# Another order of the calls on all four compute engines of a fused two-layer kernel

## The reference: what is computed

```
x = LN(x + RG_LRU(x))      x = LN(x + FFN0(x))      x = LN(x + SSM(x))      x = LN(x + FFN1(x))

RG_LRU:  c = causal 4-tap depthwise conv(x);  r, i = sigmoid(c Wr), sigmoid(c Wi)
         a = a_base ** (8 r);  b = sqrt(1 - a*a) * (i * c)
         h[t] = a[t] h[t-1] + b[t]  (by cumulated, clipped logarithms)
         out = rmsnorm(h out_w) * norm_w
FFN:     relu(x W1 + b1) W2 + b2,  256 -> 1024 -> 256
SSM:     xi, z = x in_proj;  c = silu(causal 4-tap conv(xi));  B, C, dt = c x_proj  (16, 16, 1)
         dt = softplus(dt w + b);  for each of 16 states n:
         h_n[t] = exp(dt A_n) h_n[t-1] + dt B_n c;   y = sum over n of C_n h_n
         out = (y * silu(z)) out_proj
```

## Time and profile before

| | |
|---|---|
| runs | 959.28, 961.75, 962.03 us, median 961.75 |
| profiled execution | 961.2 us, its span 959.4 us |
| granted TensorE clock, mean | 0.916 |
| PE busy | 796.9 us, 83%, 2802 matmuls |
| DVE busy | 802.2 us, 84%, 1013 instructions |
| ACT busy | 671.6 us, 70%, 1345 instructions |
| POOL busy | 561.4 us, 59%, 468 instructions |

### The profile page before, as it was taken

The page is one execution under the profiler, slowest core; times in us unless marked ns, Lnnn a source line. Parts: engine busy times, 40 slices in busy tenths (PEclk is TensorE's granted clock), DMA queues, the critical chain, the costliest instruction groups (busy, mean ns, idle before and its releaser), DMA issues. The chain is left out here.

```text
span 959.4 us, 9608 instructions
## 1 busy us (share of the span) xinstructions
PE 796.9 (83%) x2802; PEld 528.2 (55%) x2802; DVE 802.2 (84%) x1013; ACT 671.6 (70%) x1345; POOL 561.4 (59%) x468
## 2 busy tenths in 40 slices
PE   2385867978987799999899999998998797787585
PEld 1264644736554556475647564756476546546464
DVE  5245566677799999999999999999999999989761
ACT  4347687588767865997699769876976685465452
POOL 0202457437836793789378937893776376565421
PEclk9597977989998889999999999999999799789597
DMA  9000000000100010001000100010000000000000
GB/s 315 12 23 22 23 1 22 1 1 0 56 1 0 1 42 13 0 1 59 8 1 1 60 1 0 1 46 0 1 1 27 1 1 1 23 0 1 22 1 22
DMA packets 10341, 19.49 MB, mean 20 GB/s; under 512 B 1457, under 2 KB 5297, under 8 KB 10289
## 3 DMA queue, kind: packets, MB, share of 16 engines
q1 hardware_dynamic: 10288, 18.88, 5.8%
HBM read 14.69 MB, written 4.19 MB: 20 GB/s over the span
## 5 line engine op out<-in xcount | busy, mean ns | idle before, releaser
L385 POOL TENSOR_TENSOR y<-y,hC 128x1024 f32<-128x1024 f32 (+3 forms) x140 | 280.1, 2001 | 77.3 <-DVE hC L1461 73.4
L1914 PE MATMUL pC<-w,hT 128*128 128x256 f32 x1024 | 232.4, 382 | 4.9 <-ACT hT L754 4.9
L819 ACT ACTIVATE dA<-dt,A_neg 128x512 f32<-128x512 f32 (+3 forms) x320 | 187.5, 630 | 54.3 <-DVE hs L1450 53.8
L1914 PEld LDWEIGHTS pC<-w,hT 128*128 128x128 f32 x1024 | 194.5, 191 | 36.7 <-issue 7.2
L1450 DVE TENSOR_TENSOR_SCAN hs<-dA,carry,pS 128x512 f32<-128x512 f32 (+3 forms) x192 | 193.4, 1008 | 18.1 <-ACT dA L819 10.4
L2037 PE MATMUL pS<-stack,sel 97*128 97x512 f32 (+3 forms) x320 | 148.0, 515 | 54.5 <-DVE hs L1450 54.0
L1435 DVE TENSOR_TENSOR pS<-u,pS 128x1024 f32<-128x1024 f32 (+3 forms) x160 | 159.8, 999 | 17.4 <-PE pS L2037 16.8
L1461 DVE TENSOR_TENSOR hC<-hs,pS 128x1024 f32<-128x1024 f32 (+3 forms) x160 | 157.5, 985 | 15.3 <-PE pS L2037 15.1
L1450 DVE TENSOR_TENSOR_SCAN hs<-dA,pS 128x512 f32<-128x512 f32 (+1 forms) x128 | 138.2, 1080 | 14.6 <-POOL carry L392 6.0
L754 ACT ACTIVATE hT<-pA,ffb_sb 128x512 f32<-128x512 f32 (+3 forms) x160 | 94.7, 599 | 59.2 <-PE pA L1907 58.9
L1907 PE MATMUL pA<-tg,w 128*128 128x512 f32 (+3 forms) x320 | 127.9, 538 | 7.7 <-ACT hT L754 6.3
(11 more groups left out here) (120 smaller groups left out, 1101.5 us busy)
## 6 DMA issues: line engine op xcount, KB each, us to landing
xt<-xT SPq DMA_DIRECT2D x6, 515.0 KB, 4.7
xtok<-x SPq DMA_DIRECT2D x6, 512.0 KB, 5.3
out<-x3b SPq DMA_DIRECT2D x6, 512.0 KB, 2.9
w<-w1a SPq DMA_DIRECT2D x1, 1024.0 KB, 8.3
w<-w2a SPq DMA_DIRECT2D x1, 1024.0 KB, 10.4
w<-w1b SPq DMA_DIRECT2D x1, 1024.0 KB, 8.3
w<-w2b SPq DMA_DIRECT2D x1, 1024.0 KB, 9.9
xt<-xT SPq DMA_DIRECT2D x2, 259.0 KB, 7.8
```

The costliest lines, as they stand in the source:

```text
L385: nc.gpsimd.tensor_tensor(y[:, :, 0:ch.T], so_far, hC[:, n % CRING, :, 0:ch.T], ALU.add).then_inc(S["y_sum"], 1)
L819: nc.scalar.activation(dA[:, k % ARING, 0:ch.T], dt[ch.side][:, h, 0:ch.T], ACT.Exp, scale=A_neg[:, h, n:n + 1]).then_inc(S["dA_ready"], 1)
L1914: mm = nc.tensor.matmul(dst[:, b * D:b * D + D], src(k, t0), w[:, k, :], start=k == 0, stop=k == nk - 1)
```

## The change

Each engine's `opening`, `entry`, `step` and `closing` get another order of their calls. The calls are the same ones with the same arguments, and the functions they call, their waits, the buffers, the loop over the steps and SP's program stay as they are. Steps -1 and 12 come out the same on all engines. In step 0 only ACT differs. The diff has 1,984 lines, nearly all of them moved calls; shown are the moves that the prediction speaks of.

ACT's `opening` (step 1; of the second half the conv and state_decay calls between the relus are left out here):

```
                 if gate is not None:
                     squares(gate)
+                if prep is not None:
+                    x_proj_high(prep)
+                if ahead is not None:
+                    conv_first(ahead)
+                if gate is not None:
                     over_rms(gate)
                 if prep is not None:
-                    x_proj_high(prep)
                     step_sizes(prep)
+                if ahead is not None:
+                    conv_tap(ahead, 1, prep)
+                if prep is not None:
                     state_decay(prep, 0)
                 if gate is not None:
                     normalize_gate(gate)
                 if prep is not None:
                     state_decay(prep, 1)
+                    state_decay(prep, 2)
                 if gate is not None:
                     to_channel_major(S["x1T_mm"], pA[0], x1T, S["x1T_ready"], gate, 0)
                     to_channel_major(S["x1T_mm"], pA[1], x1T, S["x1T_ready"], gate, 1)
-                if prep is not None:
-                    state_decay(prep, 2)
-                if ahead is not None:
-                    conv_first(ahead)
-                if gate is not None:
                     relu(0, gate, 0, tail)
-                if ahead is not None:
-                    conv_tap(ahead, 1, prep)
-                if gate is not None:
...
```

DVE's `entry`, around the recurrence (steps 2 and 3):

```
-                        state_output(scan, 2)
-                        state_scan(scan, 3, 1)
-                        state_input(scan, 4)
-                        state_scan(scan, 4, 0)
                         state_output(scan, 3)
                         state_scan(scan, 4, 1)
                         state_input(scan, 5)
-                if gate is not None:
-                    gate_input(gate)
-                if scan is not None:
                     state_scan(scan, 5, 0)
                     state_output(scan, 4)
                     state_scan(scan, 5, 1)
                     state_input(scan, 6)
-                if gate is not None:
+                    state_scan(scan, 6, 0)
+                    state_output(scan, 5)
+                if gate is not None:
+                    gate_input(gate)
                     scaled_input(gate)
-                    recurrence(gate)
-                if scan is not None:
-                    state_scan(scan, 6, 0)
-                if prep is not None:
-                    z_silu(prep, 0)
-                    z_silu(prep, 1)
-                if scan is not None:
-                    state_output(scan, 5)
+                if scan is not None:
                     state_scan(scan, 6, 1)
                     state_input(scan, 7)
                     state_scan(scan, 7, 0)
+                if gate is not None:
+                    recurrence(gate)
+                if prep is not None:
+                    z_silu(prep, 0)
+                    z_silu(prep, 1)
+                if scan is not None:
                     state_output(scan, 6)
                     state_scan(scan, 7, 1)
...
```

PE's `entry` (steps 2 and 3) moves out_proj1, and PE's `step` (4 to 9) moves the gate products; the order of the calls there, with the spreads that lie between left out:

```
 def entry(ahead, gate, prep, scan, tail):
     down(0, prep, 1, 0)
     down(0, prep, 1, 1)
     gate_mm(gate, 0, 0)
-    out_proj1(tail, prep)
     gate_mm(gate, 0, 1)
     gate_mm(gate, 1, 0)
     gate_mm(gate, 1, 1)
+    out_proj1(tail, prep)
     x2_transpose(prep, 0, gate)
...
 def step(ahead, gate, prep, scan, tail):
+    gate_mm(gate, 0, 0)
+    gate_mm(gate, 0, 1)
     down(0, prep, 1, 0)
     down(0, prep, 1, 1)
-    gate_mm(gate, 0, 0)
-    gate_mm(gate, 0, 1)
     gate_mm(gate, 1, 0)
     out_proj1(tail, prep)
     gate_mm(gate, 1, 1)
```

DVE's `step` (4 to 9), its first calls, with the ladder's calls left out:

```
 history(prep)
-add_ffn0(prep, 0, tail)
-add_ffn0(prep, 1, tail)
 readout(tail, gate)
 clip_log_decay(gate)
-add_ssm(tail, 0)
+add_ffn0(prep, 0, tail)
 log_A(gate)
+add_ffn0(prep, 1, tail)
+add_ssm(tail, 0)
+add_ssm(tail, 1)
 a2_minus_1(gate)
-add_ssm(tail, 1)
```

More of the change, by code:

```diff
@@ L921, in entry @@
                 if scan is not None:
-                    if scan.i > 0:
-                        state_decay(scan, 4)
+                    state_decay(scan, 6)
+                if tail is not None:
+                    x3_channel_major(tail, 0, gate)
                 if gate is not None:
@@ L935, in entry @@
                 if tail is not None:
-                    x3_channel_major(tail, 0, gate)
                     x3_channel_major(tail, 1, gate)
-                if scan is not None:
-                    state_decay(scan, 6)
                 if prep is not None:
@@ L990, in entry @@
                 if scan is not None:
+                    state_decay(scan, 13)
+                    state_decay(scan, 14)
+                if gate is not None:
+                    relu(0, gate, 0, tail)
+                    relu(0, gate, 1)
+                    relu(0, gate, 2)
+                if ahead is not None:
+                    conv_tap(ahead, 2, prep)
+                if gate is not None:
+                    relu(0, gate, 3)
+                    relu(0, gate, 4)
+                if tail is not None:
+                    row_squares(LN_OUT, tail, x3b, x3)
@@ L996, in entry @@
                 if gate is not None:
+                    relu(0, gate, 0, tail)
+                if ahead is not None:
+                    conv_tap(ahead, 2, prep)
+                if gate is not None:
                     relu(0, gate, 1)
-                    relu(0, gate, 2)
                 if scan is not None:
@@ L1018, in entry, with closing @@
                     conv_tap(ahead, 3, prep)
-            def step(ahead, gate, prep, scan, tail):
-                if tail is not None:
-                    seed_x3(tail)
+            def closing(ahead, gate, prep, scan, tail):
                 if scan is not None:
@@ L1025, in step @@
                     state_decay(scan, 1)
-                    state_decay(scan, 2)
+                if tail is not None:
+                    seed_x3(tail)
                 if prep is not None:
@@ L1102, in step @@
                     relu(1, tail, 6)
-                if gate is not None:
-                    over_rms(gate)
-                if tail is not None:
-                    relu(1, tail, 7)
-                if ahead is not None:
-                    conv_first(ahead)
-                if prep is not None:
-                    x_proj_high(prep)
-                if ahead is not None:
-                    conv_tap(ahead, 1, prep)
-                if scan is not None:
-                    state_decay(scan, 10)
-                    state_decay(scan, 11)
@@ L1559, in entry @@
                         state_input(scan, 2)
+                        state_scan(scan, 2, 0)
+                if tail is not None:
+                    readout(tail, gate)
+                if scan is not None:
+                    if scan.i > 0:
+                        state_output(scan, 1)
                 if prep is not None:
@@ L1574, in entry @@
                         state_scan(scan, 3, 0)
+                        state_output(scan, 2)
+                        state_scan(scan, 3, 1)
+                        state_input(scan, 4)
+                        state_scan(scan, 4, 0)
+                if tail is not None:
+                    add_ssm(tail, 0)
                 if gate is not None:
@@ L1702, in step @@
                 if scan is not None:
+                    state_scan(scan, 3, 0)
+                if gate is not None:
+                    a2_minus_1(gate)
+                if scan is not None:
+                    state_output(scan, 2)
+                    state_scan(scan, 3, 1)
                     state_input(scan, 4)
@@ L1769, in step @@
                     state_input(scan, 13)
+                    state_scan(scan, 13, 0)
+                    state_output(scan, 12)
+                    state_scan(scan, 13, 1)
+                    state_input(scan, 14)
                 if tail is not None:
@@ L1879, in closing @@
                 if tail is not None:
+                    add_ffn1(tail, 0)
                     if tail.nj == 2:
@@ L2118, in opening @@
                 if gate is not None:
+                    down(0, gate, 0, 0, tail=tail)
                     down(0, gate, 0, 1)
@@ L2148, in entry @@
                     gate_mm(gate, 1, 1)
+                if tail is not None:
+                    out_proj1(tail, prep)
+                if scan is not None:
+                    if scan.i > 0:
+                        spread_C(scan, 3)
                 if prep is not None:
```

783 lines of the change are left out of this document (384 added, 399 removed).

## The result

| | before | after |
|---|---|---|
| median of the runs | 960.51 us (4 runs) | 984.74 us (4 runs, 984.43 to 986.02) |
| ratio | | 1.0255, 95% interval 1.0232 to 1.0278 |
| span of the profiled execution | 959.4 us | 982.6 us |
| busy PE / DVE | 796.9 / 802.2 us | 801.0 / 817.7 us |
| busy ACT / POOL | 671.6 / 561.4 us | 674.3 / 567.7 us |

The forecast was 965.7 us in a range of 953 to 974. The direction was right, the size was not: +24 us instead of +4. The calls are the same, and yet DVE is busy for 15.5 us more. That is the first thing to see: a part of the loss is not in waits at all, but in instructions that take longer.

The account below looks back on a forecast made before the run. No engine is full overall: DVE's work bounds steps 4 to 9, the gate chunk's chain steps 1 to 3. Terms 2.9 + 1.5 - 0.7 + 1.4 + 1.0 - 2.2 = +3.9 us gave a median of 965.7 us, range 953 to 974.

Parts of the forecast that it names:

- Step 0 and DVE's opening edit: ACT's conv_first moves into a wait for POOL; DVE's conv_early move does nothing: 0 for both.
- Step 1: ACT calls moved before over_rms, state_decay(0) and the x1T copies delay the copies and up0: +2.9 us (1.5 to 3.5).
- Step 2: DVE ladder calls before recurrence start it 2.2 us later; out_proj0 and its followers +1.5 us (0 to +3).
- Step 3: Later out_proj1 puts +2.1 us on recurrence; slack before out_proj0 swallows it and gives some back: -0.7 us (-2 to +2).
- Step 4: On PE two gate products move ahead of the last down products, so add_ffn0(1) waits: +1.4 us (0 to 3.5).
- Steps 5 to 9: Middle steps: moved readout, mconv_silu and spreads bring small waits, +0.2 us a step, +1.0 in all (-3 to +6).
- DVE beside POOL: Recurrence scans overlapping a POOL add take 2.05 us more; meetings shift, taken as 0 (-2.05 to +4.1).
- the sign of being wrong: The forecast is wrong if step 4's first DVE instruction precedes 258.8 us or a middle step differs by over 1 us.
- Steps 10 and 11: Earlier state_decay calls on ACT remove waits of 1.45 and 3.89 us: -2.2 us (-4 to 0).
- Rival A: DVE's ladder backlog sets steps 1 to 3, so removed waits count whole: 8.3 us less, 953.4 us; chance 0.25.
- Rival B: No change: step 3's out_proj0 slack swallows the carried 4.4 us, closing gives 2.2 back: about 961.8 us; chance 0.22.
- Rival C: The middle breaks: add_ffn0(1) waits 1.4 us in each of steps 5 to 9: 971.7 us; chance 0.15.

Follow-up runs that it names:

- e12: The kernel before with the new order of `opening` on ACT alone: 966.44 us, 1.0040.
- e1: The kernel before with the new order of `step` (steps 4 to 9) on all four engines: 978.85 us, 1.0193.
- e10: The kernel before with one call moved: ACT's mconv_tap(prep, 2) in `step` before state_decay(7), relu 2 and relu 3: 970.96 us, 1.0091.
- e3: The changed kernel, with POOL waiting in steps 4 to 9 for the gate chunk's recurrence before mconv_add(prep, 2): 988.71 us, 1.0292.
- e15: The changed kernel with POOL's conv_add(ahead, 2) back behind sum_states(9) and ACT's mconv_tap(prep, 2) behind state_decay(7) again: 982.94 us, 1.0223.
- e4: The changed kernel with POOL's conv_add(ahead, 2) in steps 4 to 9 back behind sum_states(9): 979.58 us, 1.0200.
- e7: The kernel before with the new order of `closing` (steps 10 to 12) on all four engines: 960.42 us, 0.9989.
- e5: The kernel before with the new order of `opening` (steps -1 to 1) on all four engines: 965.96 us, 1.0051.
- e6: The kernel before with the new order of `entry` (steps 2 and 3) on all four engines: 963.97 us, 1.0034.
- e9: The changed kernel with e4's edit, e3's wait with save_carry(5) ahead of it, and DVE's mconv_silu and x_proj_low at their old places: 1000.34 us, 1.0403.

## Why the prediction was wrong

Point by point, PE's row at the same call in both traces giving the shift:

- **Step 0 and DVE's opening edit, 0:** right; the first gate product of step 1 is at +0.28 us.
- **Step 1, +2.9:** measured +3.5 at the next gate product, of which 2.25 at over_rms and 0.6 more at the x1T copies, by the steps given (e12: ACT alone is the cause). The 5.09 us wait at 98.96 went, as forecast, and bought nothing; up's last product lost 1.0 more than its first, as ACT's relu stretch now has state_decay(3) and (4) in it.
- **Step 2, +1.5:** out_proj0 came 1.74 us later than the carried 3.5, recurrence 2.25 later, close to the 2.2. But the first down product of the next chunk is again at +3.5, so the step added 0. A row says where 1.0 us of it went: out_proj0 took 5.37 us, not 6.37.

```profile
132.61 2.53 DVE L1394 TENSOR_TENSOR_SCAN st<-decay,st,tg 128x512 f32<-128x512 f32 x2
```

```profile
135.84 5.37 PE L1915 MATMUL pC<-out_w,st 128*128 128x256 f32 x16 [2.51 <-DVE zz L1412]
```

- **Step 3, -0.7:** measured +0.4. The recurrence was 5.3 us later than the carried shift (8.77 - 3.5), the upper end that I had named, and 1.05 us longer; out_proj0 (223.05) had no slack left. The relus and up then gave most of it back.
- **Step 4, +1.4:** step 5 starts at +4.07 on DVE and +0.66 on PE, so it added nothing. Add_ffn0(1) did not wait there; it did once, 0.59 us, in step 6.
- **Steps 5 to 9, +1.0 (-3 to +6), and the term "DVE beside POOL", 0 (-2.05 to +4.1):** measured +19.5 together, from 4.07 to 23.58. This is the step that failed. I had the right row and the right price (2.05 us), and then let the meetings come and go at random, "two more" at most, with 0 as the term. But steps 5 to 8 are one schedule repeated, and the add met the recurrence in each of them, also in e1. Four more meetings are 8.05 us of longer scans. E10, with five more of them in the old order, shows the price in time, 8.7 us; in the new order taking them away (e3, e15) did not give it back. To see it I would have had to follow mconv_tap(prep, 2) on ACT, which the new order makes before state_decay(7), to the moment at which the add starts, and compare that with the recurrence in the row. The rest of DVE's 15 us of longer instructions in these steps lies mostly at scaled_input (three longer by 0.5 to 1.5), dt_x (1.19 in step 6) and history (1.41 in step 9). In the trace each of them starts while POOL is in an instruction and ends after it: scaled_input in step 5 (1.75 us from 403.55) beside a sum_states until 404.21 and in step 9 beside mconv_add, dt_x beside conv_add(ahead, 2), and history beside a sum_states.
- **The same steps, POOL's order:** the forecast for them went by moves of DVE and PE alone and did not follow conv_add(ahead, 2), the longest move on POOL. It costs 5.2 us (e4).
- **The same steps, their length:** the forecast gave 95.2 to 95.5 us for each. That was misread: by the step starts above, the kernel before has 95.67, 95.91, 94.66, 93.34 and 88.03. The changed kernel has 99.25, 101.01, 101.29, 95.29 and 90.28, so the sign of being wrong, over 1 us in a middle step, came in each.
- **The same steps, the clock:** out_proj0 in steps 6 and 7 takes 5.41 and 6.74 us after PE had stood idle for 2.72 and 2.73, and 3.62 in the same steps of the kernel before, without an idle before it; the granted clock over the two long products was 0.68 and 0.54, and x_proj_low then waits 1.30 and 2.54. The granted clock over steps 4 to 9 fell from 0.96 to 0.95. The row's releaser is z_silu (zz), of which the second now stands behind the blocked recurrence. That the blocked recurrence makes the idle is shown by e3 and e15: with the scans at 2.46 us PE is idle for 0.73 to 0.75 us before out_proj0 in steps 5 to 7, the product takes 3.72 or 3.73, and x_proj_low does not wait in steps 5 to 8. This is the mechanism that I had weighed for step 2 by the Trainium skill, page "TensorE: Matmul & The Clock Gate", section "HAM oscillation — how this bites in real kernels", in the wrong step: in step 2 the longer idle came with a shorter product (5.37 for 6.37), in steps 6 and 7 with a longer one. In step 5 of the changed kernel 2.74 us of idle left it at 3.72, and in e1 the same idle gave 5.41 in step 5 and 3.72 in steps 6 and 7, so idle alone does not decide it.

```profile
410.49 3.72 PE L1915 MATMUL pC<-out_w,st 128*128 128x256 f32 x16 [2.74 <-DVE zz L1412]
```

- **Steps 10 and 11, -2.2:** measured -0.3 in the changed trace and -1.2 alone (e7). The waits of 1.45 and 3.89 us went (0.50 us is left), and others grew, as 2.01 at add_ssm; the end hangs on the same serial chain, 13.66 us at the last add_ffn1.

Rival A, by which ladder calls ahead of the gate work would save 8 us, fell in every part: no wait of DVE's taken from steps 1 to 3 came back as time (e5, e6 are slower). Rival B's sum took the 2.4 us of slack in step 3 twice, since the -0.7 holds it already; in the runs that slack gave nothing back (e5). Rival C named the right steps, but for a wait at add_ffn0(1) that came once.

What stays open is how the new `step`'s +18.4 us divide. Some 8 can be put to the blocked recurrences and 5 to conv_add(ahead, 2); 3.8 lie in the x_proj_low waits, of which e4 keeps 1.30 and 1.33, so that these overlap with the 5. But apart from e4's 5.2 us these are sizes in one trace, and e3, e15 and e9 show that taking one away in the new order returns it, with interest, at mconv_silu, save_carry or state_decay(9). How much each would be worth in an order built around it wasn't found.

## What to carry to other kernels

In a pipeline whose middle steps repeat, price a collision times the number of repetitions, not as an accident: one row of 4.51 us beside 2.46 was worth 8.7 us once a single moved call brought it into each step (e10). For every call that is moved, follow what it releases on the other engines, above all on the engine that nobody looks at: one POOL add, late by 20 us, cost 5 us in one order of ACT and 32 in another, depending on what is queued behind its waiter. And the lists of the four engines are one schedule: exchanging a single engine's list cost some 106 us over the changed kernel (130.2 above before instead of 24.2), and a repair on one engine must be followed through the queues of the other three.

## What the runs showed of the hardware

In these traces a DVE instruction that reads two tiles of SBUF and a POOL instruction on SBUF tiles do not run together: the one that starts second is the longer by most of what is left of the other. With POOL's add 0.16 us ahead the two scans of a recurrence take 4.46 us for 2.46, all of it in the first scan (3.28 for 1.28); with the add 0.38 ahead they take 4.36 (e10), and with POOL held until after them 2.46 (e3). An add that starts 0.57 us into the first scan is stretched to 2.85 us for 2.36 and still costs DVE 2.05 us, now at the second scan (4.51 in all). An add that comes during the second scan costs DVE nothing, and it is POOL that takes longer (2.64 for 2.36, in the kernel before). What had kept the kernel before free in steps 5 to 7 was thus a start of the add 1.85 us or more behind the first scan. The same holds for scaled_input (3.37 for 1.22 with the add 0.06 us ahead, e10) and mconv_silu (2.28 for 1.29, e15), while state_input and state_output, which read one of their tiles from PSUM, took 1.19 to 1.23 us in all calls of 1024 columns, in the kernel before and in the changed one. The Trainium skill, page "SBUF — State Buffer", section "🔬 SBUF: two separate sides", says that the two share one port pair as a lock, that the one that starts first has it for its whole instruction, and that the other is blocked; the rows of e3 and e10 agree with it.
